# Layer 0 mixing: batch 0 multiplied ahead of turning batch 1's y, and the recurrence's states read by ScalarE in place of GpSimd

## What is computed

```python
h = _ln(x, ln1_g, ln1_b); hs = _shift(h, time_shift)
k, v, r = hs @ Wk, hs @ Wv, hs @ Wr
def step(carry, kv_t):                      # over the 512 rows, elementwise per channel
    p = jnp.maximum(pp, u + kk); e1 = jnp.exp(pp - p); e2 = jnp.exp(u + kk - p)
    y = (e1 * aa + e2 * vv) / (e1 * bb + e2)
    ww_kk = w + kk; pu = jnp.maximum(pp + w, ww_kk)
    e1u = jnp.exp(pp + w - pu); e2u = jnp.exp(ww_kk - pu)
    aa_n = e1u * aa + e2u * vv; bb_n = e1u * bb + e2u
    return ((aa_n, bb_n, pu + jnp.log(bb_n)), y)
x = x + sigmoid(r) * y
h2s = _shift(_ln(x, ln2_g, ln2_b), time_shift)
x = x + sigmoid(h2s @ Wcr) * (jnp.square(relu(h2s @ Wck)) @ Wcv)
```

## Time and profile before

| what | value |
|---|---|
| median of three executions | 3730.09 us |
| the profiled execution | 3736.8 us |
| its span, first to last instruction | 3735.1 us |
| busy over the span: TensorE / VectorE / ScalarE / GpSimd | 3113.4 / 2164.9 / 1367.2 / 1428.5 us |
| mean granted TensorE clock (1 is full) | 0.899 |
| the mixing phase: VectorE's first work, TensorE's last matmuls end, VectorE's last work ends | 692.1, 1064.7, 1073.7 us |
| busy from 690 to 1073.7 us: TensorE / VectorE / ScalarE / GpSimd | 283.3 / 295.9 / 107.8 / 191.4 us |

### The profile page before, as it was taken

How to read it: one execution, slowest core, us unless ns; L and a number is a source line. 1 busy time by engine, 2 the same in 40 slices (tenths; PEclk the granted TensorE clock), 3 DMA queues, 4 the chain that set the end, 5 groups by cost and what they waited for, 6 DMA issues and landing times. The chain is left out here.

```text
span 3735.1 us, 46452 instructions
## 1 busy us (share of the span) xinstructions
PE 3113.4 (83%) x14629; PEld 1859.0 (50%) x14629; DVE 2164.9 (58%) x6568; ACT 1367.2 (37%) x3094; POOL 1428.5 (38%) x1013
## 2 busy tenths in 40 slices
PE   7732999398769999799999999697998757989888
PEld 4422666266435555444444445374665434555554
DVE  4552999889644442446666655521221356888777
ACT  4421555242226666234434443221232143334331
POOL 1435000166605444021112211124003379899883
PEclk9865999699879999989999998787999878999988
DMA  5562444233230000100000000312223110000000
GB/s 198 194 218 98 125 125 125 96 105 95 81 118 1 1 1 1 40 6 18 18 18 18 18 12 12 110 44 86 63 85 91 48 47 1 6 12 6 6 6 12
DMA packets 138093, 221.08 MB, mean 59 GB/s; under 512 B 12801, under 2 KB 106241, under 8 KB 137089
## 3 DMA queue, kind: packets, MB, share of 16 engines
q1 hardware_dynamic: 99040, 146.92, 11.9%
q0 software_dynamic: 18432, 50.36, 4.3%
q10 hardware_dynamic: 20384, 20.84, 1.7%
HBM read 107.45 MB, written 110.62 MB: 58 GB/s over the span
## 5 line engine op out<-in xcount | busy, mean ns | idle before, releaser
L2297 DVE CUSTOM_DVE_ANT_0 a_ps_s<-a_ps_s,a_hide_row,a_fmax 128x384 f32<-128x384 f32 (+3 forms) x512 | 249.5, 556 | 172.8 <-PE a_ps_s L2004 172.6
L3578 POOL TENSOR_TENSOR c_prod<-c_att,c_v 128x2048 f32<-128x2048 f32 x64 | 287.3, 4528 | 29.9 <-DVE c_att L3638 29.9
L2209 POOL TENSOR_SCALAR_AFFINE_SELECT a_probs<-a_probs 128x512 f32<-128x512 f32 x128 | 79.7, 635 | 567.7 <-ACT a_probs L2486 567.7
L3578 POOL TENSOR_TENSOR c_prod<-c_q,c_k 128x2048 f32<-128x2048 f32 x64 | 286.7, 4515 | 17.5 <-ACT c_k L3989 13.5
L1505 POOL TENSOR_TENSOR a_probs<-a_probs,a_causal 128x512 f32<-128x512 f32 (+1 forms) x96 | 157.3, 1650 | 216.0 <-ACT a_probs L1734 216.0
L1734 ACT ACTIVATE a_probs<-a_ps_s 128x512 f32<-128x512 f32 (+1 forms) x384 | 170.7, 538 | 120.0 <-PE a_ps_s L1374 119.9
L3412 PE MATMUL c_side<-c_w_e,c_h2T 128*128 128x512 f32 x448 | 205.5, 615 | 1.0 <-DVEq L3785 1.0
L2486 ACT ACTIVATE a_probs<-a_ps_s 128x512 f32<-128x512 f32 (+1 forms) x384 | 171.9, 538 | 90.8 <-PE a_ps_s L2026 90.3
L2688 PE MATMUL b_ps_y<-b_w_ff,b_gelu 128*128 128x256 f32 x512 | 130.8, 407 | 60.6 <-issue 59.2
L703 PE MATMUL p_side<-p_w_expert,p_sortedT 128*128 x636 | 179.7, 407 | 0.0
L1018 POOL TENSOR_TENSOR p_inv<-k_scan,p_ones 128x512 f32<-128x512 f32 x16 | 20.7, 1292 | 386.0 <-ACT p_bonus L1156 345.1
(11 more groups left out here) (508 smaller groups left out, 7309.1 us busy)
## 6 DMA issues: line engine op xcount, KB each, us to landing
p_sorted_in<-sorted_scratch SPq DMA_DIRECT2D x39, 512.0 KB, 4.8
y_scratch<-p_y_out SPq DMA_DIRECT2D x39, 512.0 KB, 3.1
sorted_scratch<-all_zero ACTq DMA_DIRECT2D x1, 12160.0 KB, 57.7
sorted_scratch<-all_zero SPq DMA_DIRECT2D x1, 9088.0 KB, 30.3
b_sorted_in<-sorted_scratch SPq DMA_DIRECT2D x17, 512.0 KB, 4.6
y_scratch<-b_y_out SPq DMA_DIRECT2D x17, 512.0 KB, 3.2
sorted_scratch<-all_zero ACTq DMA_DIRECT2D x1, 8192.0 KB, 32.0
all_x_res<-x SPq DMA_DIRECT2D x8, 512.0 KB, 5.2
```

Source lines behind the costliest of these rows:

```text
L2297: last = nc.vector.tensor_tensor_reduce(out=there, in0=there, in1=hide_row[:, (TT - 1 - t) * P:], scale=HD ** -0.5, scalar=fmax[i % 2][:, ...
L3578: nc.gpsimd.tensor_tensor(out, left[:, heads].broadcast_to([P, HALF, HEADS, HD]), right.broadcast_to([P, HALF, HEADS, HD]), ALU.mult).then ...
```

## The change

The reads leave GpSimd: ScalarE does them as an Identity activation with the bias 1 or bonus, in the order inv's two halves, signal, den's two halves, signal, and values waits for one signal before each of its reciprocals. On ScalarE, read_q(0) and read_q(1) come first, read_q(i+2) after the first four squares of batch i; rows_normalised(1) moves behind gate_rows(0). TensorE multiplies batch 0 (up, receptance) before it turns batch 1's y, and from batch 1 on it turns y of batch i+1 in the middle of up(i) instead of after down(i-1). VectorE's finish(i-1) comes before new_rows(i+1).

```diff
@@ -939,10 +939,11 @@
                         last = nc.tensor.transpose(ps[:, t * P:(t + 1) * P], hn[:, t, k * P:(k + 1) * P], ident[:])
                     last.then_inc(side.filled("hn", i, k), 1)
 
-            def up(i):
-                for k in range(KD):
-                    pe.wait_ge(*side.when_freed("hn", i, k))
-                for n in range(NF):
+            def up(i, first, end):
+                if first == 0:
+                    for k in range(KD):
+                        pe.wait_ge(*side.when_freed("hn", i, k))
+                for n in range(first, end):
                     ps = side.take("kk", i, n)
                     pe.wait_ge(*side.bank_free("kk", i, n))
                     for k in range(KD):
@@ -975,16 +976,21 @@
 
             turn_y(0)
             turn_hn(0)
+            pe.wait_ge(weights_in, ONE + 3 * DMA)
+            up(0, 0, NF)
+            receptance(0)
             turn_y(1)
-            pe.wait_ge(weights_in, ONE + 3 * DMA)
-            for i in range(B):
-                up(i)
+            down(0)
+            turn_hn(1)
+            for i in range(1, B):
+                up(i, 0, NF // 2)
+                if i + 1 < B:
+                    turn_y(i + 1)
+                up(i, NF // 2, NF)
                 receptance(i)
                 if i + 1 < B:
                     turn_hn(i + 1)
                 down(i)
-                if i + 2 < B:
-                    turn_y(i + 2)
 
         @block.sync
         def _(sp):
@@ -1012,14 +1018,6 @@
         @block.gpsimd
         def _(pool):
 
-            def read_q(i):
-                pool.wait_ge(y_ready, ONE + i)
-                for k in range(KD):
-                    nc.gpsimd.tensor_tensor(inv[:, k, :], q_at(i, k, 0), ones[:, 0:1].broadcast_to([P, T]), ALU.add)
-                    last = nc.gpsimd.tensor_tensor(den[:, k, :], q_at(i, k, 0),
-                                                   bonus[:, k:k + 1].broadcast_to([P, T]), ALU.add)
-                last.then_inc(q_read, 1)
-
             def shifts(i):
                 if i:
                     pool.wait_ge(hn_ready, ONE + i)
@@ -1040,13 +1038,8 @@
                             bass.IndirectOffsetOnAxis(ap=keep.slot_int[:, n, TT * i + t:TT * i + t + 1], axis=0)
                             ).then_inc(gathered[i], DMA)
 
-            pool.wait_ge(setup_done, ONE + 4)
-            read_q(0)
-            read_q(1)
             shifts(0)
             for i in range(B):
-                if i + 2 < B:
-                    read_q(i + 2)
                 if i + 1 < B:
                     shifts(i + 1)
                 gather(i)
@@ -1059,13 +1052,14 @@
             nc.vector.memset(ones[:], 1.0).then_inc(setup_done, 1)
 
             def values(i):
-                dve.wait_ge(q_read, ONE + i + 1)
+                dve.wait_ge(q_read, ONE + 2 * i + 1)
                 dve.wait_ge(v_in, ONE + DMA * (i + 1))
                 nc.vector.reciprocal(inv[:], inv[:]).then_inc(chain, 1)
                 dve.wait_ge(chain, ONE + CHAIN * i + 1)
                 for k in range(KD):
                     last = nc.vector.tensor_tensor(inv[:, k, :], inv[:, k, :], q_at(i, k, 1), ALU.mult)
                 last.then_inc(chain, 1)
+                dve.wait_ge(q_read, ONE + 2 * i + 2)
                 nc.vector.reciprocal(den[:], den[:]).then_inc(chain, 1)
                 dve.wait_ge(chain, ONE + CHAIN * i + 2)
                 for k in range(KD):
@@ -1137,11 +1131,10 @@
             measure(0)
             values(1)
             for i in range(B):
+                if i:
+                    finish(i - 1)
                 if i + 1 < B:
                     new_rows(i + 1)
-                if i:
-                    finish(i - 1)
-                if i + 1 < B:
                     measure(i + 1)
                 if i + 2 < B:
                     values(i + 2)
@@ -1155,6 +1148,14 @@
             act.wait_ge(cols_in, ONE + DMA)
             nc.scalar.activation(bonus[:], cols[:, :, 3], ACT.Exp).then_inc(setup_done, 1)
             act.wait_ge(setup_done, ONE + 4)
+
+            def read_q(i):
+                act.wait_ge(y_ready, ONE + i)
+                for out, shift in ((inv, ones[:, 0:1]), (den, None)):
+                    for k in range(KD):
+                        last = nc.scalar.activation(out[:, k, :], q_at(i, k, 0), ACT.Identity,
+                                                    bias=bonus[:, k:k + 1] if shift is None else shift)
+                    last.then_inc(q_read, 1)
 
             def rows_normalised(i):
                 act.wait_ge(shift_ready, ONE + i + 1)
@@ -1202,14 +1203,20 @@
                     act.wait_ge(rr_ready, ONE + 2 * i + half + 1)
                     act.sem_inc(side.freed("rr", i, half), 1)
 
+            read_q(0)
+            read_q(1)
             rows_normalised(0)
             columns(0)
             for i in range(B):
                 squares(i, 0, NF // 2)
-                if i + 1 < B:
+                if i + 2 < B:
+                    read_q(i + 2)
+                if 0 < i < B - 1:
                     rows_normalised(i + 1)
                 squares(i, NF // 2, NF)
                 gate_rows(i)
+                if i == 0:
+                    rows_normalised(1)
                 if i + 1 < B:
                     columns(i + 1)
 
```

More of the change, by code:

```diff
@@ L1139, in _ @@
             for i in range(B):
-                if i + 1 < B:
-                    new_rows(i + 1)
                 if i:
@@ L1144, in _ @@
                 if i + 1 < B:
+                    new_rows(i + 1)
                     measure(i + 1)
```

## The result

The changed kernel takes 3698.5 us (median of four, 3697.35 to 3701.71) against 3729.9 for the kernel before on the same chip (four, 3727.91 to 3733.07). The ratio is 0.9913, 95% interval 0.99 to 0.9927: 31.4 us faster, inside the forecast range of 3684 to 3716 and 4.5 us under the 3703 forecast.

The account below looks back on a forecast made before the run. VectorE was taken to bound the mixing loop (39.44 us busy of 40.10). Gains of 6.5 at the start and 21.5 in the loop, less 1 for short pauses, make 27 us: 3730 to 3703 us, range 3684 to 3716.

Parts of the forecast that it names:

- Reads leave GpSimd: Mixing loop: four VectorE combines fall from 12.0 to 6.7 us, the period from 40.1 to 34.8; gain 21.5 us.
- Reads on ScalarE: Mixing loop: strided reads take 1.1 us each, 4.4 a batch, fit with 2 us left; cost nothing up to 1.6 each.
- the rival (ScalarE's read in the way): Mixing loop: reads over 1.6 us delay down, whole gain gone at 2.7 us; chance 0.04 together with any other loss.
- The first read: Start of mixing: VectorE's 5.21 us wait for the first reads shortens with two signals; gain 2.3 us, bounds 1.7 to 3.0.
- TensorE's order at the start: Start of mixing: up(0) runs 18.4 us earlier, values(3) starts at 782.6 instead of 789.15; gain 6.5 us, first read's 2.3 included.
- The order in the loop: Mixing loop: TensorE round trip 34.5 us, 0.3 under VectorE's 34.8, so the period is 34.8.
- Short pauses: Mixing loop: short TensorE pauses after runs of 16 gathers now count; 1 us lost in all, bounds 0 and 12.
- The rival in which the pauses hold TensorE's period: Mixing loop: pauses after 16 gathers grow to 2 to 3 us in six batches, 10 to 16 us lost; chance 0.17.
- The long pause: TensorE's 24 us pause in down(6), beside 32 unbroken gathers, moves along with them; costed at no change.
- the rival in which the long pause changes: Pause in down(6) shrinks or vanishes if it depends on TensorE's program place; up to 24 us more gain, 3679; chance 0.15.

Follow-up runs that it names:

- the dearer reads: Changed kernel plus four more ScalarE reads of the states into a spare tile behind each batch's four: 3728.3 us, ratio 1.0007.
- the kernel with only the reads: Kernel before with the states read by ScalarE, one signal each, all orders of VectorE and TensorE unchanged: 3704.75 us, ratio 0.9948.
- spaced pair: Kernel before and changed kernel, both with the last mixing gathers held back and layer 2's gather groups each awaiting the previous landing: 3683.5 and 3656.95 us.
- the kernel with the short break: Changed kernel with the last batch's gathers waiting only until the 16 of batch 6 have landed: 3692.3 us, ratio 0.9908.
- the kernel with GpSimd's writes: Changed kernel plus four GpSimd memsets into a spare tile behind the gathers of batches 1 to 4: 3694.2 us, ratio 0.9914.

## Why the prediction came out

*Reads leave GpSimd.* Right, and shown both ways. All eight combines take 6.8 us, four periods 139.6 us against 139.2 forecast (values(3) 781.78, values(7) 921.40): 21.1 of the 21.5 us.

*Reads on ScalarE.* The price was right: 1.1 us each. The row that shared the stride was the right one to take, not the contiguous 0.62. By the Trainium skill's rule on 16-byte lines (SBUF — State Buffer, "Door 1: The DMA port swizzle") the stride should cost; the trace agrees, 1.16 us a read against 0.62. The room was read rightly as well: 2 us forecast, 1.69 measured, and with twice the reads the delay alone costs 2.4 us a period, which is the prediction's own bill for 2.2 us a read (four times the 0.6 above 1.6). What the bill left out is that a later hn idles TensorE and lowers its clock, 1.7 to 2.7 us more in every period, and that 7.1 us go at the start. So the rival (ScalarE's read in the way) was priced too cheaply: the whole gain is gone at 2.2 us, where the prediction had 2.7.

*The first read.* VectorE's wait fell from 5.21 to 2.38 us, 2.8 us against 2.3 and inside the bound of 3.0. The first reciprocal moved by more, from 697.51 to 694.12, because the phase began 0.6 us earlier. v had landed in time.

*TensorE's order at the start.* Right in each step: up(0) at 728.11 (forecast 729.3), turn_y(1) at 747.42 (748.5), new_rows(1) at 748.15 after 5.91 us (749.7 after 6), new_rows(2) at 777.42 (778.2), values(3) at 781.78 (782.6): 7.4 us against 6.5, and 6.8 without the earlier begin of the phase.

*The order in the loop.* 34.7 us against 34.8, and VectorE busy 34.10 of 34.69. The round trip was put too long: where VectorE waits for it, new_rows comes 0.73 us behind the start of turn_y (812.24 to 812.97), where the prediction counted 0.9 + 0.4; where it doesn't wait, 1.56 us (880.80 to 882.36, lines below). The difference, 0.8 us, is the slack; the prediction had 0.3.

*Short pauses.* 1 us was allowed and 0.9 was lost in the first of the four periods, but that is luck: no pause took it. down(1) ran 15.77 us instead of 14.08, its first 3.24 us at a granted clock of 0.58, after TensorE had waited 2.37 us for ScalarE's squares. These 1.7 us less the slack of 0.8 are the 0.9. Timelines of TensorE and VectorE, and the stretch at the low clock:

```profile
789.76 15.77 PE L973 MATMUL p_side<-p_w_cv,p_kk 128*128 128x256 f32 x64 [2.37 <-ACT p_kk L1186]
...
812.97 1.29 DVE L1090 TENSOR_TENSOR p_x<-p_side,p_xn 128x512 f32<-128x512 f32 x2 [0.77 <-PE p_side L929]
...
880.80 1.03 PE L929 MATMUL p_side<-all_ident,p_y 128*128 128x128 f32 x8
...
789.76:793.00 3.24, 3.23 (x9) 2.59 (x10) 3.24 (x2) 2.37 (x4) 2.36 (x3) 0.58 0.29 85
```

Five of the experiments have the same loop, and their four periods take 138.7 to 138.8 us, with nothing lost. A real pause shows once, ahead of the loop: TensorE idles 2.61 us ahead of up(1) with nothing to wait for, and new_rows(2) waits 1.21. The rival in which the pauses hold TensorE's period did not come.

*The long pause.* "The pause of 24 us moves with them and I cost it at no change": in the trace this term is off. Up to combine(5) the gain is 28.6 us (984.63 to 956.07), at combine(6) 28.7 (1034.58 to 1005.87), at the last combine 33.3. In the kernel before TensorE left the slow stretch still in down(6), and up(7) began at 1032.19, 2.4 us ahead of combine(6). In the changed kernel the stretch begins 19.2 us behind the first gather of the run (958.48), not 16.2 (987.0, 1003.2), when down(6) has 4 matmuls left, and 8 of up(7)'s 32 pass inside it:

```profile
982.57 0.59 PE L973 MATMUL p_side<-p_w_cv,p_kk 128*128 128x256 f32 x1 [1.01 <-issue]
984.68 1.01 PE L950 MATMUL p_side<-p_hT,p_w_ck 128*128 128x512 f32 x1 [1.52 <-issue]
...
988.87 1.01 PE L950 MATMUL p_side<-p_hT,p_w_ck 128*128 128x512 f32 x1 [1.79 <-issue]
...
1002.17 3.42 PE L950 MATMUL p_side<-p_hT,p_w_ck 128*128 128x512 f32 x4 [0.39 <-issue]
```

It resumes 3.7 us ahead of combine(6) with those 8 behind it: 1.3 us, and 8 x 0.43 = 3.4 (16 take 7.03 elsewhere), are the 4.6. Of 24.5 us some 20 are lost, where the prediction moved 24 along.

That the change did this is not shown. From combine(5) to the last combine the kernel before takes 82.3 us and the changed one 77.5. Five experiments whose last 32 gathers also run unbroken take 75.1 to 76.2 (78.0 with the dearer reads). One of them is the kernel with only the reads, whose orders are those of the kernel before; its VectorE timeline:

```profile
966.17 6.79 DVE L1117 SCALAR_TENSOR_TENSOR all_x_res<-k_rows,k_gate,all_x_res 128x256 f32<-128x256 f32 x16
...
1041.28 6.79 DVE L1117 SCALAR_TENSOR_TENSOR all_x_res<-k_rows,k_gate,all_x_res 128x256 f32<-128x256 f32 x16
```

So the 24 us of the one trace of before may be that execution's own; it lay 6.7 us above its median. The spaced pair needs 58.7 and 58.4 us for the same part, so without the stretch the change makes nothing there. What the change gives in the phase apart from the stretch is 28 us (to combine(5)) to 29 us (the spaced pair), where 27 was forecast; the 33.3 of the trace hold 4.7 of the slow stretch besides, and the rival in which the long pause changes is neither shown nor excluded.

## What to carry to other kernels

When two engines share a loop, the room an instruction has is the idle time printed beside its successor plus the slack of the loop (1.7 + 0.8 us here); past that, count what the delay does to the next engine's clock too, which here doubled the bill. GpSimd's reads of SBUF were paid for by the two-input VectorE instruction beside them (5.3 us for 5.05), and an engine that looks idle is the right home for it only if the queue there reaches the read in time, which here took the other half of the change. And a matmul chain that crawls with "issue" as its only reason is worth a look at what GpSimd issues at that time: holding gathers apart was worth 40 us on the kernel before, more than the change. Compare starts within a phase from its first work: it moved by up to 3 us between kernels that do the same work ahead of it.

## What was not expected of the hardware

TensorE is slowed by a run of indirect DMAs on GpSimd, 1.25 us each. The slowing begins some 13 to 18 gathers into an unbroken run (before, changed, and the second run of the kernel with the short break; 20 or so in one run of layer 2) and ends 2 to 5 us behind the last. Inside, the granted clock falls to 0.58, TensorE's matmuls start at steps of 0.7 us or multiples of it (978.35, 979.07, 981.17, 982.57), whatever their width, and the other engines learn of them late. VectorE takes up down(6)'s second half at 1003.83, after 21.87 us of waiting, though its last matmul stands at 982.57. Its first half it takes up 16.8 us behind down's start (964.48 to 981.27), where down(7) has 7.2 (1017.46 to 1024.64): the signal of a half that was done by some 972 is late. In the kernel with GpSimd's writes it comes at 976.94, 12.6 us behind down's start and before TensorE slows at 978.6. Timelines of TensorE and VectorE:

```profile
964.48 13.22 PE L973 MATMUL p_side<-p_w_cv,p_kk 128*128 128x256 f32 x60 [2.08 <-ACT p_kk L1186]
...
981.27 0.69 DVE L1107 TENSOR_TENSOR p_rr<-p_side,p_rr 128x512 f32<-128x512 f32 x1 [18.40 <-remote]
1003.83 0.69 DVE L1107 TENSOR_TENSOR p_rr<-p_side,p_rr 128x512 f32<-128x512 f32 x1 [21.87 <-remote]
```

After a break of 2.6 us TensorE is quick again and the count begins anew, though ScalarE stayed late; layer 2's groups of 8 with breaks show no slow stretch. What runs short (instructions, semaphore updates, a queue that the gathers fill) stays open: no run here separates them. The Trainium skill (SBUF — State Buffer, "Who interferes with whom") says that TensorE and ScalarE never wait on anyone. That is about ports of SBUF; the time of both says that they can be held by something beside them.
